# A weight set-up moved into the recurrence's first chunk, a router moved between expert products, and a reciprocal written to PSUM, in an eight-stage hybrid model on one core

## The chip, the cores and the metric

The program runs on one core of a Trainium2 chip, as one launch. The metric is the device time of one execution in microseconds (us), lower is better. Names used below: PE is TensorE, DVE is VectorE, ACT is ScalarE, POOL is GpSimd, SP is SyncE, which issues most DMAs.

## The reference

One sequence of 2048 tokens with 128 features, float32, goes through eight residual stages, each of the form `x = x + f(layernorm(x))`:

```
x = x + rwkv6(ln(x))              # 16 heads of 8: gated linear recurrence over 2048 steps
x = x + moe_top2(ln(x))           # 8 experts, hidden 256, exact gelu, b2 per expert
x = x + rope_attention(ln(x))     # causal, 16 heads of 8
x = x + moe_top2(ln(x))           # the same weights again
x = x + full_attention(ln(x))     # 1 head of 128, not causal
x = x + perturbed_ffn(ln(x))      # 8 experts, 7 of them alike, softmax router
x = x + latent_attention(ln(x))   # causal, 8 heads of 128 over 2 latents of 32
x = x + perturbed_ffn(ln(x))
```

The top-2 router is `softmax((h @ Wg + bg) / 5)`, the two largest kept and divided by their sum. The perturbed weights need the k-th smallest and largest absolute value of four tensors.

## The kernel before, in words

Tokens lie in 16 tiles of 128 (`NT`), or 4 chunks of 512 (`NC`, `CH`). X stays in SBUF for the whole program. Each stage is a class with one method for each engine; `build` makes a list of stages, and each engine runs its method of stage after stage in that list. So an engine's instructions stand in the order of the list, and engines meet only at semaphores. PSUM has eight banks, which the stages share by number (`k.bank(7)`).

**The recurrence** (`Rwkv`) goes over the 4 chunks and in each over 8 columns j. DVE makes a product with the replicated values (`kvj`), a scan (`state`) and a product with r (`rsj`); PE replicates the values for column j + 2 and sums `rsj` into bank 6. At j = 5 PE also projects the next chunk. Bank 7 serves the group norm of the chunk before (centre, variance, spread, output), and is not used in chunk 0. ACT copies the projections out (`take`), with a change of table between sigmoid and exp.

**Later weights** (`LaterWeights`) prepare what later stages read: 15 transposes of 128 x 128 on PE (the qkv weights, the padded output weights, `wq`), two small ones, and the products `wc` and `wy`; ACT copies each group from PSUM. DVE splits the rows of b2 into three bfloat16 parts on three partitions (`split_rows`) and makes four strided copies for the rotated qkv weights. In the list this stage stands behind the recurrence, so every engine comes to it when the recurrence is done. DVE's layer norm of the first expert stage stands behind it. GpSimd's part of it runs early, at 32 us, and GpSimd then waits for the recurrence to end, and starts a bisection of 31 rounds (`Perturb`) that runs beside the next stages.

**Experts** (`Experts`, `Router`). In each chunk PE does, for e = 0 to 7, the hidden products of expert e (2 products, banks 0 to 3) and the output of expert e - 1 (a seed from the b2 rows, then 8 products, banks 4 and 5). ACT applies gelu. DVE adds the gated output to X. The router stands ahead of that as its own stage: 16 narrow products into bank 7, then some two dozen small DVE instructions and one exp on ACT, to the gates. PE waits until DVE has read the logits before it goes on.

**Latent attention** (`CausalHeads` with `summed`). A plan made at build time interleaves on PE the scores of key tile after key tile with "ring" items, which pass through banks 5 to 7: maxima ahead of time, turns, sums, outputs. DVE works the ring items in the same order. The softmax denominators are sums over keys of exp(scores): for each unit GpSimd adds the weights of heads 0 to 2 to an accumulator in SBUF, DVE those of head 3 (line 1533). At the end of each of the 8 (quad, chunk) pairs PE sums the accumulator over partitions into a ring bank, DVE takes the reciprocal (line 1641) into SBUF, and multiplies it with the output `O` (line 1643).

The profile counts lines of this kernel: 202, 221, 227 layer norm; 468 to 485 later weights on PE; 495 to 505 their copies on ACT; 516, 524 to 530 the DVE part; 737, 792, 809 the recurrence on DVE; 989, 994, 1001 hidden, seed and output products; 1053 the gated addition; 1085 the router's products; 1375, 1611 maxima.

Of the kernel before, what the change touches and what calls it, by code (L numbers as in the profile page):

```python
# [22 lines left out]
P = 128  # L23
# [232 lines left out]
class Setup(Stage):  # L256
# [43 lines left out]
    def alloc(self, ctx):  # L300
# [14 lines left out]
        self.row0 = sb("row0", [3, 8, P])  # L315
        self.rowr = sb("rowr", [3, 8, P])
        self.rowb = sb("rowb", [3, 8, P], BF16)
        self.n_loaded, self.n_rest = (16 * len(x) for x in self.loads())

    def loads(self):  # L320
# [29 lines left out]
        load(self.row0[:, :, :], d["L0_ffn_b2"].rearrange("(a e) d -> a e d", a=1).broadcast_to([3, 8, P]))  # L350
# [79 lines left out]
class LaterWeights(Stage):  # L430


    def __init__(self, k):
        self.k, self.setup = k, k.setup
        self.turned = self.setup.turned
        self.copied = [k.sem(f"later_copied{i}") for i in range(2)]
        self.ready = k.sem("later_ready")


    def groups(self):  # L440
        k, s = self.k, self.setup
        pads = [s.wpad[:, g, :, :].rearrange("p j c -> p (j c)") for g in range(4)]
        return [([s.wraw[:, i, :] for i in range(5, 8)], k.wqkvT[:, 0:3, :]),
                (pads, k.woutT[:, :, :]), ([s.wq[:, i, :] for i in range(4)], s.wqT[:, 0:4, :]),
                ([s.wq[:, i, :] for i in range(4, 8)], s.wqT[:, 4:8, :])]

    def gpsimd(self, g):
        k, s = self.k, self.setup
        g.wait_ge(s.loaded_rest, s.n_rest)
        g.wait_ge(s.loaded, s.n_loaded)  # L450
        g.wait_ge(s.zeroed, s.n_zeroed)
        g.tensor_copy(s.wpad[:, :, :, 0:8], s.wraw[:, 8, :].rearrange("p (g j d) -> p g j d", g=4, j=4)) \
            .then_inc(self.ready, 1)
        g.tensor_copy(k.identb[:, :], k.ident).then_inc(self.ready, 1)
        g.tensor_copy(k.mask_qk[:, :], k.cst[:, (5 + 8) * P:(6 + 8) * P]).then_inc(self.ready, 1)
        g.tensor_copy(k.mask_kq[:, :], k.cst[:, (6 + 8) * P:(7 + 8) * P]).then_inc(self.ready, 1)

    def tensor(self, pe):
        k, s = self.k, self.setup
        pe.wait_ge(s.loaded_rest, s.n_rest)  # L460
        pe.wait_ge(s.ready, 1)
        pe.wait_ge(self.ready, 4)
        n = 0
        for ins_, _ in self.groups():
            if n >= 2:
                pe.wait_ge(self.copied[n % 2], n // 2)
            for i, a in enumerate(ins_):
                ins = pe.transpose(k.PS[:, 4 + n % 2, i * P:(i + 1) * P], a, k.ident)
            ins.then_inc(self.turned[n % 2], 1)
# [12 lines left out]

        for h in range(8):
            g, j = h // 4, h % 4
            ins = pe.matmul(k.PS[32 * j:32 * j + 32, 4, g * P:(g + 1) * P], s.wvupT[:, :], s.wo[:, h, :],
                            start=True, stop=True)
        ins.then_inc(self.turned[0], 1)

    def scalar(self, act):
        k, s = self.k, self.setup  # L490
        n = 0
        for _, out in self.groups():
            act.wait_ge(self.turned[n % 2], n // 2 + 2)
            w = out.shape[1]
# [1725 lines left out]
```

## Time and profile before

| | us |
|---|---|
| median of 3 runs | 1803.63 |
| the runs | 1799.49, 1803.63, 1818.74 |
| the profiled execution | 1799.15 |
| its span, first to last instruction | 1797.3 |

The stages in the trace: set-up and recurrence to 161.5 us, first experts 161.5 to 326, rope attention to 880, second experts to 1030, full attention to 1230, first perturbed experts to 1340, latent attention to 1711, second perturbed experts to the end. Over the span PE is busy 1578.2 us, DVE 1127.0, ACT 772.4, POOL 753.4. A share of the whole span says little here, since each stage has its own limit; a change is read in its own stage. A granted clock of 1.00 is 2.4 GHz on TensorE, 0.50 is 1.2 GHz.

### The profile page before, as it was taken

The numbers are of one execution on the slowest core, as the hardware profiler recorded it, in microseconds if no ns is written. First come the engines' busy times: TensorE is split into PE (matmuls) and PEld (weight loads), VectorE is DVE, ScalarE is ACT, GpSimd is POOL, SyncE is SP. The second block draws the span as 40 slices with busy tenths as digits, with TensorE's granted clock in tenths as the row PEclk, the third lists the DMA queues.
The fourth block names the chain that finished last, engine by engine and source line by source line (L and its number), as shares of the span: only waits on it lengthen the run. The fifth ranks groups of instructions, "written<-read, shape, count | busy, mean of one in ns | idle before, by whom it ended". The sixth has DMA issues, their size and how long they took to land.

```text
span 1797.3 us, 25837 instructions
## 1 busy us (share of the span) xinstructions
PE 1578.2 (88%) x8927; PEld 810.0 (45%) x8927; DVE 1127.0 (63%) x2330; ACT 772.4 (43%) x1007; POOL 753.4 (42%) x955
## 2 busy tenths in 40 slices
PE   5885999689999899999799879989879889898689
PEld 2333666333333344343366547776634333333256
DVE  6778333798788787884233333334378978787941
ACT  2321333615565555656433334444344334344443
POOL 0003636454554536363645454600004546667800
PEclk9997899859999999999799989997979889899879
DMA  5000000323001010000000000000062000000000
GB/s 149 0 1 1 1 1 0 116 55 54 2 16 41 2 45 12 2 2 2 1 1 1 0 0 1 0 0 1 0 183 56 23 23 2 1 0 2 0 7 18
DMA packets 39124, 36.90 MB, mean 21 GB/s; under 512 B 10190, under 2 KB 36271, under 8 KB 38898
## 3 DMA queue, kind: packets, MB, share of 16 engines
q1 hardware_dynamic: 36826, 28.48, 5.6%
q10 hardware_dynamic: 2136, 7.10, 2.0%
q8 instruction: 62, 1.02, 0.2%
q14 instruction: 36, 0.29, 0.1%
q0 software_dynamic: 64, 0.00, 0.0%
HBM read 26.10 MB, written 8.91 MB: 19 GB/s over the span
## 4 chain that ended last, share of the span: by engine, by line
PE 70%; DVE 14%; issue 3%; ACT 3%; POOL 2%; DMA 1%; SPq 0%; DVEq 0%; POOLq 0%; ACTq 0%
PE PS L1427 11%; PE PS L1001 10%; PE PS L1375 10%; PE PS L1446 10%; PE PS L989 10%; PE PS L1875 3%; PE PS L1893 3%; DVE sb_rope_mp L1611 3%; POOL sb_H L1533 2%; DVE sb_latent_mp L1611 2%; DVE sb_latent_rec L1641 1%; PE PS L1887 1%; PE PS L994 1%; PE PS L1085 1%; PE PS L1404 1%
## 5 line engine op out<-in xcount | busy, mean ns | idle before, releaser
L1611 DVE TENSOR_REDUCE sb_rope_mp<-PS 128x1 f32<-128x512 f32 (+3 forms) x560 | 344.5, 668 | 67.7 <-PE PS L1379 33.3
L1488 ACT ACTIVATE sb_rope_PT<-PS 128x1024 f32<-128x1024 f32 (+3 forms) x320 | 273.3, 895 | 212.3 <-PE PS L1431 114.2
L1053 DVE SCALAR_TENSOR_TENSOR sb_X<-PS,sb_gates,sb_X 128x128 f32 (+1 forms) x320 | 90.2, 344 | 238.4 <-PE PS L1001 238.2
L1375 PE MATMUL PS<-sb_rope_K,sb_rope_Q 96*128 96x512 bf16 (+3 forms) x640 | 212.8, 372 | 7.6 <-ACT sb_rope_V L1473 6.5
L1611 DVE TENSOR_REDUCE sb_latent_mp<-PS 128x1 f32<-128x512 f32 (+2 forms) x280 | 175.6, 668 | 36.7 <-PE PS L1375 26.9
L593 POOL TENSOR_SCALAR sb_pbelow<-sb_pa,sb_ptrial 128x512 f32<-128x512 f32 x124 | 194.0, 1575 | 6.4
L600 POOL TENSOR_TENSOR sb_pbelow<-sb_pbelow 128x1024 f32<-128x1024 f32 (+1 forms) x248 | 182.4, 735 | 19.6
L989 PE MATMUL PS<-sb_HT,sb_w 128*128 (+1 forms) x384 | 181.9, 611 | 3.6 <-DVE sb_seed L528 1.9
L1427 PE MATMUL PS<-sb_rope_Q,sb_rope_K 99*128 99x512 bf16 (+3 forms) x640 | 181.1, 354 | 1.4 <-ACT sb_rope_PT L1488 0.9
L1427 PE MATMUL PS<-sb_latent_Q,sb_latent_K 96*128 96x512 bf16 (+7 forms) x640 | 158.8, 369 | 5.3 <-ACT sb_w0b L1488 2.4
L1030 ACT ACTIVATE sb_moe_hidden<-PS,sb_vec 128x512 f32<-128x512 f32 x128 | 87.5, 687 | 158.7 <-PE PS L989 154.6
L1446 PE MATMUL PS<-sb_rope_PT,sb_rope_V 128*9 128x512 f32 (+3 forms) x1280 | 150.0, 541 | 0.1
L1375 PE MATMUL PS<-sb_latent_K,sb_latent_Q 96*128 96x512 bf16 (+3 forms) x320 | 106.8, 382 | 30.7 <-DVE sb_latent_mp L1611 22.6
L1375 PEld LDWEIGHTS PS<-sb_rope_K,sb_rope_Q 96*128 96x128 bf16 x640 | 59.9, 100 | 161.8 <-issue 83.2
L1001 PE MATMUL PS<-sb_w0b,sb_moe_hidden 128*128 128x128 f32 x1024 | 131.3, 281 | 0.0
L1001 PEld LDWEIGHTS PS<-sb_w0b,sb_moe_hidden 128*128 128x128 f32 x1024 | 119.1, 191 | 14.5 <-issue 14.5
L989 PEld LDWEIGHTS PS<-sb_HT,sb_w 128*128 128x128 f32 x384 | 70.2, 197 | 69.5 <-issue 65.5
L606 POOL TENSOR_TENSOR sb_ptot<-sb_ptot,sb_prank 128x8 f32<-128x8 f32 x31 | 6.1, 197 | 223.0 <-issue 223.0
L1427 PEld LDWEIGHTS PS<-sb_latent_Q,sb_latent_K 99*128 99x128 bf16 (+1 forms) x640 | 58.2, 102 | 82.3 <-issue 20.7
L605 POOL PARTITION_ALL_REDUCE sb_ptot<-sb_pcnt x31 | 13.2, 426 | 187.2 <-issue 187.2
L1427 PEld LDWEIGHTS PS<-sb_rope_Q,sb_rope_K 99*128 99x128 bf16 x640 | 59.3, 100 | 69.7 <-issue 18.3
L1531 POOL COPY sb_pbelow<-sb_w 128x1536 f32<-128x1536 f32 x3 | 4.4, 1462 | 189.6 <-ACT sb_w L1488 181.9
(322 smaller groups left out, 2622.3 us busy)
## 6 DMA issues: line engine op xcount, KB each, us to landing
sb_latent_Q<-latent_parts SPq DMA_DIRECT2D x48, 128.0 KB, 2.8
sb_rope_Q<-rope_parts ACTq DMA_DIRECT2D x9, 384.0 KB
rope_parts<-sb_rope_parts SPq DMA_DIRECT2D x24, 128.0 KB, 2.4
latent_parts<-sb_latent_parts SPq DMA_DIRECT2D x12, 256.0 KB, 2.7
sb_rope_tab<-in_rotation SPq DMA_DIRECT2D x1, 2048.0 KB, 8.2
sb_rope_K<-rope_parts ACTq DMA_DIRECT2D x6, 256.0 KB
latent_parts<-sb_latent_parts SPq DMA_DIRECT2D x12, 128.0 KB, 2.4
sb_latent_K<-latent_parts SPq DMA_DIRECT2D x48, 32.0 KB, 2.2
```

What stands on the lines that cost most here:

```text
L593: ch.mark(g.tensor_scalar(self.below[:, w, s, :], self.a[:, w, :], tr[:, 2 * w + s:2 * w + s + 1], None, ALU.is_lt))
L600: ch(g.tensor_tensor(bl[:, :, 0:n], bl[:, :, 0:n], bl[:, :, n:2 * n], ALU.add))
L989: pe.matmul(k.bank(b), self.w1(e, m), x, start=True, stop=True).then_inc(self.hid[b], 1)
L1001: ins = pe.matmul(k.PS[:, 4 + b, i * P:(i + 1) * P], self.g[:, b, m, i * P:(i + 1) * P], self.w2(e, m), start=False, stop=(m == M - 1), sk ...
L1030: s.activation(self.g[:, e % 2, m, :], k.bank(b), self.func, bias=self.b1(e, m)) \
L1053: ins = v.scalar_tensor_tensor(xi, k.PS[:, 4 + b:5 + b, i * P:(i + 1) * P], gate, xi, ALU.mult, ALU.add)
L1375: ins = pe.matmul(k.PS[:, bank, at:at + w], self.Q[0:self.rows, g % 2, j, 0, q0:q0 + P], self.K[0:self.rows, g % 2, j % self.kheads, 0, kc ...
L1427: ins = pe.matmul(k.PS[:, j, q0:CH], self.K[0:r, g % 2, j % self.kheads, m, kj * P:(kj + 1) * P], self.Q[0:r, g % 2, j, m, c * CH + q0:(c ...
L1446: ins = pe.matmul(k.PS[32 * j:32 * j + self.vcols, 4, q0:CH], v, self.PT[u % self.B][:, j, q0:CH], start=(kj == 0), stop=(kj == last))
L1488: s.activation(self.PT[u % self.B][:, 2 * p:2 * p + 2, q0:CH], k.PS[:, 2 * p:2 * p + 2, q0:CH], ACT.Exp, scale=self.scale).then_inc(self.e ...
L1611: v.tensor_reduce(self.mp[:, n % 2, kc, heads[0]:heads[-1] + 1, i], k.PS[:, bank, 0:len(heads) * w].rearrange("p (h k) -> p h k", h=len(he ...
L1875: ins = pe.matmul(k.bank(c), self.qi[:, b, :], self.kT[:, c * CH:(c + 1) * CH], start=True, stop=True)
```

## The change

It has three parts.

1. **Later weights.** The stage is now ahead of the recurrence in the list, but has no PE, ACT or DVE method of its own. The recurrence calls `turn(pe, n)` and `copy(act, n)` in chunk 0: groups 0 to 3 on PE behind the columns 2 to 5, group 4 (`wc` and `wy`) behind column 7; ACT copies groups 0 to 3 ahead of `take(1)` and group 4 behind it. All go through bank 7, so each group waits for the copies of the one before, and the centring of chunk 1 waits for the last copy. The rotated qkv weights come from two more ACT copies. The b2 rows are split on GpSimd (5 instructions on 8 partitions) and brought to their three partitions by three DMAs from GpSimd's queue; the experts wait for these.
2. **Router.** In the two top-2 stages the router's products stand inside the experts' first turn on PE, behind the hidden products of expert 1, and its exp on ACT behind the gelus of expert 1. The wait for the logits to be read is gone.
3. **Latent reciprocal.** It is written over its own input in PSUM, and the multiplication reads it there. The bank is given back behind the multiplication, not behind the reciprocal.

```diff
 class LaterWeights(Stage):
+    FIRST = 5
+    LAST = 2
...
+    def before_group(self, n):
+
+        return 0 if n == 0 else self.FIRST + n - 1
+
+    @property
+    def all_copied(self):
+        return self.before_group(4) + self.LAST
 
     def gpsimd(self, g):
...
+        ch(g.tensor_copy(s.rowb[:, 0, :], s.row0[:, :]))
+        ch(g.tensor_tensor(s.row0[:, :], s.row0[:, :], s.rowb[:, 0, :], ALU.subtract))
+        ch(g.tensor_copy(s.rowb[:, 1, :], s.row0[:, :]))
+        ch(g.tensor_tensor(s.row0[:, :], s.row0[:, :], s.rowb[:, 1, :], ALU.subtract))
+        ch(g.tensor_copy(s.rowb[:, 2, :], s.row0[:, :]))
+        for r in range(3):
+            g.dma_start(k.seed0[r:r + 1, :, :], s.rowb[:, r, :]).then_inc(self.seeded, 16)
...
+    def turn(self, pe, n):
+        k, s = self.k, self.setup
+        if n == 0:
+            pe.wait_ge(s.loaded_rest, s.n_rest)
+        else:
+            pe.wait_ge(self.copied, self.before_group(n))
+        if n == 1:
+            pe.wait_ge(self.padded, 1)
+        if n == 4:
+            pe.wait_ge(self.padded, 4)
+        if n < 4:
...
+            for i, a in enumerate(blocks):
+                ins = pe.transpose(k.PS[:, 7, i * P:(i + 1) * P], a, k.ident)
...
+        ins.then_inc(self.turned, 1)
...
-    def vector(self, v):
-        k, s, ch = self.k, self.setup, Chain(v, self.setup.steps, self.setup.STEPS)
-        v.wait_ge(s.loaded_rest, s.n_rest)
-        split_rows(ch, v, s.row0[:, :, :], s.rowr[:, :, :], s.rowb[:, :, :], k.seed0[:, :, :], k)
-        v.wait_ge(self.copied[0], 1)
-
-        for i in range(2):
             for a in range(2):
-                ch(v.tensor_copy(k.wqkvT[:, 3 + i, :].rearrange("p (m a) -> p m a", a=2)[:, :, a:a + 1],
-                                 k.wqkvT[:, i, :].rearrange("p (m a) -> p m a", a=2)[:, :, 1 - a:2 - a]))
+                act.activation(k.wqkvT[:, 3:5, :].rearrange("p i (m a) -> p i m a", a=2)[:, :, :, a:a + 1],
+                               full[:, 0:2, :].rearrange("p i (m a) -> p i m a", a=2)[:, :, :, 1 - a:2 - a],
+                               ACT.Copy).then_inc(self.copied, 1)
...
@@ Rwkv.scalar, the end
             if c:
                 centre(c)
                 deviation(c)
+            else:
+                for n in range(4):
+                    k.later.copy(s, n)
             if c + 1 < NC:
                 take(c + 1)
+            if c == 0:
+                k.later.copy(s, 4)
@@ Rwkv.tensor
             pe.wait_ge(self.o_sb, m)
             if m > 1:
                 pe.wait_ge(self.ready, m - 1)
+            else:
+                pe.wait_ge(k.later.copied, k.later.all_copied)
...
+                if c == 0 and 2 <= j <= 5:
+                    k.later.turn(pe, j - 2)
+                if c == 0 and j == 7:
+                    k.later.turn(pe, 4)
@@ Experts
-        if not self.between:
-            for sem, val in self.router.banks_free():
-                pe.wait_ge(sem, val)
...
+                if first and e == 1 and not self.between:
+                    self.router.project(pe)
...
+                if first and e == 1 and not self.between:
+                    self.router.exponents(s)
@@ CausalHeads.dve_item, "sum", summed
-                v.reciprocal(self.rec[:, :], k.bank(bank)).then_inc(free, 1)
-                v.wait_ge(free, uses + 1)
-                v.tensor_tensor(self.On[:, n % 2, :], self.O[:, n % 2, :], self.rec[:, :], ALU.mult) \
-                    .then_inc(self.normed, 1)
+                ch(v.reciprocal(k.bank(bank), k.bank(bank)))
+                ch(v.tensor_tensor(self.On[:, n % 2, :], self.O[:, n % 2, :], k.bank(bank), ALU.mult))
+                v.sem_inc(self.normed, 1)
+                v.sem_inc(free, 1)
```

TensorE at the end of chunk 0 and the start of chunk 1 of the recurrence, before (`wvrep` are the value products, `rsj` the sums, `centring` and `sq` the group norm, `rk` the bonus):

```order
L890 MATMUL PS<-sb_rw_mixv,sb_wvrep 128x512
L938 MATMUL PS<-sb_rw_rsj,sb_cst 128x512
L890 MATMUL PS<-sb_rw_mixv,sb_wvrep 128x512
L938 MATMUL PS<-sb_rw_rsj,sb_cst 128x512
L896 MATMUL PS<-sb_rw_o,sb_centring 128x512
L901 MATMUL PS<-sb_cst,sb_rw_sq 128x16 x4
L928 MATMUL PS<-sb_rw_rk,sb_cst 128x512
```

The same place now:

```order
L896 MATMUL PS<-sb_rw_mixv,sb_wvrep 128x512
L946 MATMUL PS<-sb_rw_rsj,sb_cst 128x512
L896 MATMUL PS<-sb_rw_mixv,sb_wvrep 128x512
L946 MATMUL PS<-sb_rw_rsj,sb_cst 128x512
L492 MATMUL PS<-sb_wkupT,sb_wqT 128x32 x8
L495 MATMUL PS<-sb_wo,sb_wvupT 32x128 x8
L904 MATMUL PS<-sb_rw_o,sb_centring 128x512
L909 MATMUL PS<-sb_cst,sb_rw_sq 128x16 x4
L936 MATMUL PS<-sb_rw_rk,sb_cst 128x512
```

Sixteen products have come ahead of the centring; they stood behind the whole recurrence before.

TensorE from the end of the recurrence to the second expert, before (`rw_z` is the recurrence's last output, `wraw` to `wo` the later weights, `H` the layer norm's transposes, `wg` the router):

```order
L914 MATMUL PS<-sb_wT,sb_rw_z 128x128 x4
L468 MATMUL PS<-sb_cst,sb_wraw 128x128 x3
L468 MATMUL PS<-sb_cst,sb_wpad 128x128 x4
L468 MATMUL PS<-sb_cst,sb_wq 128x128 x8
L474 MATMUL PS<-sb_cst,sb_wup 128x32 x2
L480 MATMUL PS<-sb_wkupT,sb_wqT 128x32 x8
L485 MATMUL PS<-sb_wo,sb_wvupT 32x128 x8
L238 MATMUL PS<-sb_cst,sb_H 128x128 x16
L1085 MATMUL PS<-sb_wg,sb_HT 128x8 x16
L989 MATMUL PS<-sb_HT,sb_w 128x512 x4
L994 MATMUL PS<-sb_seed,sb_onesb 128x512
L1001 MATMUL PS<-sb_w0b,sb_moe_hidden 128x128 x8
```

And now:

```order
L922 MATMUL PS<-sb_wT,sb_rw_z 128x128 x4
L238 MATMUL PS<-sb_cst,sb_H 128x128 x16
L998 MATMUL PS<-sb_HT,sb_w 128x512 x4
L1108 MATMUL PS<-sb_wg,sb_HT 128x8 x16
L1003 MATMUL PS<-sb_seed,sb_onesb 128x512
L1010 MATMUL PS<-sb_w0b,sb_moe_hidden 128x128 x8
```

The later weights are gone from here, and the router and the first four hidden products have changed places.

VectorE around the second denominator of latent attention, now (`mp` are maxima, `pbelow` the accumulator of head 3):

```order
L1631 TENSOR_REDUCE sb_latent_mp<-PS 128x1 x2
L1661 RECIPROCAL PS<-PS 128x512
L1662 TENSOR_TENSOR sb_latent_On<-sb_latent_O,PS 128x512
L1631 TENSOR_REDUCE sb_latent_mp<-PS 128x1 x2
L1553 TENSOR_TENSOR sb_pbelow<-sb_pbelow,sb_w 128x512
L1631 TENSOR_REDUCE sb_latent_mp<-PS 128x1 x4
```

The order is that of before; the reciprocal's output and the multiplication's second input are in PSUM.

## Rows read from the trace of the kernel before

**Rows 1.** The page: its span, and the chain's shares by engine.

```profile
span 1797.3 us, 25837 instructions
...
PE 70%; DVE 14%; issue 3%; ACT 3%; POOL 2%; DMA 1%; SPq 0%; DVEq 0%; POOLq 0%; ACTq 0%
```

**Rows 2.** Timeline, VectorE, layer norms and recurrence's tail: start, duration, engine, line, operation.

```profile
13.98 4.19 DVE L227 TENSOR_SCALAR sb_H<-sb_X,sb_mv,sb_rstd 128x128 f32<-128x128 f32 x16
...
160.82 0.69 DVE L769 TENSOR_TENSOR sb_X<-sb_X,PS 128x512 f32<-128x512 f32 x1 [2.16 <-PE PS L914]
161.42 0.67 DVE L524 CAST sb_rowb<-sb_row 3x1024 bf16<-3x1024 f32 x1
...
171.88 0.87 DVE L202 BATCH_NORM_STATS2 sb_stats<-sb_X 128x6 f32<-128x128 f32 x4
...
174.48 6.06 DVE L227 TENSOR_SCALAR sb_H<-sb_X,sb_mv,sb_rstd 128x128 f32<-128x128 f32 x16
```

**Rows 3.** Timeline, the recurrence's chunks 0 and 1, then the later weights.

```profile
31.95 1.22 POOL L454 CAST sb_identb<-sb_cst 128x128 bf16<-128x128 f32 x1
...
58.74 1.12 PE L896 MATMUL PS<-sb_rw_o,sb_centring 128*128 128x512 f32 x2 [0.78 <-DVE sb_rw_o L742]
...
64.56 0.69 DVE L737 TENSOR_TENSOR sb_rw_kvj<-sb_rw_k,PS 128x512 f32<-128x512 f32 x1 [0.83 <-PE PS L890]
...
162.96 0.66 PE L468 MATMUL PS<-sb_cst,sb_wq 128*128 128x128 f32 x4 [0.24 <-ACT sb_woutT L495]
...
164.48 2.65 PE L480 MATMUL PS<-sb_wkupT,sb_wqT 128*128 128x32 f32 x16 [0.63 <-ACT sb_wvupT L500]
...
167.06 1.08 PE L485 MATMUL PS<-sb_wo,sb_wvupT 128*32 128x128 f32 x16
167.16 0.38 ACT L502 ACTIVATE sb_wc<-PS 128x256 f32<-128x256 f32 x1 [2.74 <-PE PS L480]
```

**Rows 4.** Timeline, the first expert stage's start.

```profile
182.40 6.99 PE L1085 MATMUL PS<-sb_wg,sb_HT 128*128 128x8 f32 x32 [0.69 <-ACT sb_HT L250]
...
189.78 5.23 PE L989 MATMUL PS<-sb_HT,sb_w 128*128 128x512 f32 x8 [0.38 <-DVE sb_rt_p L1102]
...
197.42 1.13 DVE L1053 SCALAR_TENSOR_TENSOR sb_X<-PS,sb_gates,sb_X 128x128 f32<-128x128 f32 x4
...
202.97 0.38 PE L994 MATMUL PS<-sb_seed,sb_onesb 3*128 3x512 bf16 x1
```

**Rows 5.** By line: count, duration ns min/median/max, first and last start, shape.

```profile
L1641 DVE RECIPROCAL sb_latent_rec<-PS x8: 3357/3357/3358, 1370.4 to 1704.0; 128x512 f32<-128x512 f32 x8
...
L1643 DVE TENSOR_TENSOR sb_latent_On<-sb_latent_O,sb_latent_rec x8: 691/3289/3800, 1373.8 to 1707.4; 128x512 f32<-128x512 f32 x8
...
L1652 DVE TENSOR_TENSOR sb_X<-sb_X,PS x24: 676/687/689, 436.8 to 1710.3; 128x512 f32<-128x512 f32 x24
```

**Rows 6.** Windows, latent attention: length, busy us of PE, PEld, DVE, ACT, POOL, granted clock.

```profile
1340.00:1711.00 371.00, 317.00 (x1937) 125.01 (x1935) 311.45 (x423) 147.53 (x170) 222.52 (x80) 0.90 0.06 18
```

**Rows 7.** Timeline, GpSimd and VectorE at the second and seventh denominators.

```profile
1393.30 3.42 POOL L1533 TENSOR_TENSOR sb_pbelow<-sb_pbelow,sb_w0b 128x1536 f32<-128x1536 f32 x1 [1.37 <-ACT sb_w0b L1488]
1393.47 3.80 DVE L1643 TENSOR_TENSOR sb_latent_On<-sb_latent_O,sb_latent_rec 128x512 f32<-128x512 f32 x1
...
1398.39 0.68 DVE L1533 TENSOR_TENSOR sb_pbelow<-sb_pbelow,sb_w 128x512 f32<-128x512 f32 x1
...
1659.36 3.95 POOL L1533 TENSOR_TENSOR sb_H<-sb_H,sb_w0b 128x1536 f32<-128x1536 f32 x1 [2.56 <-ACT sb_w0b L1488]
```

**Rows 8.** Windows (columns as in the group of latent attention); the sum is of five low stretches.

```profile
1393.90:1397.90 4.00, 0.04 (x1) 0.00 (x0) 4.00 (x3) 0.00 (x0) 2.82 (x1) 0.99 0.00 0
...
1656.60:1658.30 1.70, 0.04 (x4) 0.00 (x0) 1.67 (x3) 1.05 (x2) 0.19 (x1) 1.00 0.00 0
...
1397.90:1404.60 6.70, 6.67 (x23) 2.18 (x23) 5.55 (x13) 2.05 (x2) 0.24 (x1) 0.50 0.00 0
...
sum 30.90, PE 30.68 PEld 10.16 DVE 22.42 ACT 9.10 POOL 5.61; mean PE 6.14 PEld 2.03 DVE 4.48 ACT 1.82 POOL 1.12
```

More of the change, by code:

```diff
@@ L430 @@
 class LaterWeights(Stage):
+    FIRST = 5
+    LAST = 2
     def __init__(self, k):
         self.k, self.setup = k, k.setup
[L435 to L445, printed above, removed]
+        k.later = self
+        self.turned = k.sem("later_turned")
+        self.copied = k.sem("later_copied")
+        self.padded = k.sem("later_padded")
+        self.pool_steps = k.sem("later_steps")
+        self.seeded = k.sem("later_seeded")
+    def before_group(self, n):
[3 more added lines that the diff above has]
+        return self.before_group(4) + self.LAST
     def gpsimd(self, g):
-        k, s = self.k, self.setup
+        k, s, ch = self.k, self.setup, Chain(g, self.pool_steps)
         g.wait_ge(s.loaded_rest, s.n_rest)
@@ new lines, in copy @@
+    def copy(self, act, n):
+        k, s = self.k, self.setup
+        act.wait_ge(self.turned, n + 1)
+        full = k.bank(7).rearrange("p (n d) -> p n d", d=P)
+        if n == 0:
+            act.activation(k.wqkvT[:, 0:3, :], full[:, 0:3, :], ACT.Copy).then_inc(self.copied, 1)
+            for a in range(2):
+                act.activation(k.wqkvT[:, 3:5, :].rearrange("p i (m a) -> p i m a", a=2)[:, :, :, a:a + 1],
+                               full[:, 0:2, :].rearrange("p i (m a) -> p i m a", a=2)[:, :, :, 1 - a:2 - a],
+                               ACT.Copy).then_inc(self.copied, 1)
+            act.activation(s.wkupT[:, :], k.PS[:, 7, 384:416], ACT.Copy).then_inc(self.copied, 1)
+            act.activation(s.wvupT[:, :], k.PS[:, 7, 416:448], ACT.Copy).then_inc(self.copied, 1)
+        elif n < 4:
+            out = (k.woutT[:, :, :], s.wqT[:, 0:4, :], s.wqT[:, 4:8, :])[n - 1]
+            act.activation(out, full, ACT.Copy).then_inc(self.copied, 1)
+        else:
+            act.activation(k.wc[:, :, :], k.PS[:, 7, 0:256].rearrange("p (h l) -> p h l", h=8), ACT.Copy) \
+                .then_inc(self.copied, 1)
+            act.activation(k.wy[:, :, :], k.PS[:, 7, 256:512].rearrange("p (h l) -> p h l", h=2), ACT.Copy) \
+                .then_inc(self.copied, 1)
@@ L1021, in scalar, with turn @@
         uses = E * M // 4
-        for sem, val in self.needs:
-            s.wait_ge(sem, val)
-        def turn(c):
+        if self.between:
+            for sem, val in self.needs:
+                s.wait_ge(sem, val)
+        def turn(c, first):
             for e in range(E):
@@ L1036, in scalar @@
         with s.Fori(1, NC) as c:
-            turn(c)
+            turn(c, False)
     def vector(self, v):
@@ L1081, in tensor, with scalar, project @@
     def tensor(self, pe):
+        if not self.inside:
+            self.project(pe)
+    def scalar(self, s):
+        if not self.inside:
+            self.exponents(s)
+    def project(self, pe):
         k = self.k
@@ L2106, in rwkv @@
             perturb.after = [(rw.ready, NC)]
[L2107 removed]
+            stages.extend([SetupCopies(k), LaterWeights(k), rw])
             return lambda c: [(rw.ready, c + 1)]
[L2110 to L2113 removed]
         def full_attention():
```

93 lines of the change are left out of this document (29 added, 64 removed).

## The prediction

> **What bounds the kernel.** I read the first lines of the page, then the chain of waits, then the stretches that the change touches as timelines, and the granted clock of a few short windows. The profiled execution took 1799.15 us for a span of 1797.3; the median of the three runs is 1803.63, so the sum below stands 4.5 under it. The chain that ended last is TensorE for 70% of the span and VectorE for 14% [rows 1]. Three stretches matter. At the end of the recurrence VectorE alone holds up the next stage: from the last addition to X to the next statistics it does twelve instructions that the next stage doesn't need [rows 2]. In the first expert stage TensorE does the router, then the hidden products. In latent attention both TensorE (317 of 371 us) and VectorE (311 of 371) are nearly full [rows 6], so there a shorter VectorE instruction can count.
>
> **1. The tail of the recurrence.** The last addition ends at 160.82 + 0.69 = 161.5, the statistics start at 171.88 [rows 2]. Between them stand the split of b2 and four copies. The change takes both from VectorE, and the statistics wait for nothing else: 10.4 us gone. TensorE's turns and ScalarE's copies lay beside them and go too. What is late next is the normalization itself.
> Given back, a: chunk 0. Four groups of about four transposes go in after j = 2 to 5, each about 0.66 us [rows 3]. VectorE sets the pace in chunk 0, and TensorE waits for it ahead of its products, so two or three groups are covered; the last stands right ahead of chunk 1's projections, behind which VectorE is the one that waits. I take one group uncovered, +0.7 (bounds 0 and 4 x 0.66 = 2.6).
> Given back, b: the last group, after j = 7: 2.65 + 1.08 us of products, then two ScalarE copies of 0.38, and the centring of chunk 1 now waits for these [rows 3]. TensorE was idle 0.78 there. 3.73 + 0.7 - 0.8 = +3.6. Behind the waiting centring stand the variance, the bonus and the value products, and VectorE already waits 0.83 us for those, so it passes through in full. Bounds: 2.0 (products at the full clock) and 5.
> Given back, c: the normalization now meets GpSimd's opening instructions. Its sixteen instructions took 4.19 us with GpSimd idle and 6.06 beside it [rows 2]; I take +1.5 on top (bounds 0 and 4).
> The b2 rows: five GpSimd instructions on 8 partitions and three DMAs on GpSimd's queue. No row shows them. The nearest is the cast of the identity, 1.22 us beside VectorE [rows 3]; eight of these, 10 us, from 31.7 on are over long before the last group at 58, and the experts need the result after 160. Nothing for it; at 3 us each they would start to hold the group. They may delay VectorE in chunk 0 by up to 0.5 us, within bound a.
> Part 1: -10.4 + 0.7 + 3.6 + 1.5 = **-4.6** (-8.4 to +1.7).
>
> **2. The router inside turn 0**, twice. Before: router 6.99 us, a wait of 0.38, hidden products 5.23, first gated addition 197.42 - 182.40 = 15.0 us after the start [rows 4]. Now the hidden products come first, and the logits come that much later: with 6.0 for the products (the clock is still low) and 4.5 for the router (between half of 6.99 and all of it), at 10.5 instead of 7.0. VectorE's chain from logits to the first addition stays 197.42 - 182.40 - 6.99 = 8.0, so the addition ends at 10.5 + 8.0 + 1.1 = 19.6. The first TensorE instruction that needs it, the seed of expert 2, began 20.6 us after the start (202.97) [rows 4]. So there is 1 us of slack and 0.38 saved. Against it stands the clock: the router's narrow products come just ahead of expert 0's, and where the clock falls behind them each stretch of 4 us costs 2. ScalarE has one more table load, beside the router. I take **+1.5** for both (-3 to +6), nearer the zero that the slack gives.
>
> **3. The latent reciprocal in PSUM.** The reciprocal takes 3.357 us in all eight cases. The multiplication behind it, both inputs in SBUF, has a median of 3.289 and a least value of 0.691; the addition of an SBUF tile and a PSUM bank of the same size takes 0.676 to 0.689 in all 24 cases [rows 5]. The timeline shows why: GpSimd starts an addition at 1393.30, and VectorE's multiplication of 0.69 runs from 1393.47 until that has ended [rows 7]. Once one input is in PSUM I expect 0.69 each time: 3.289 - 0.687 = 2.6 us of VectorE at each of five chunks, some 0.5 at the first, where GpSimd's instruction is short, nothing at the last, where GpSimd is done. No row shows a reciprocal that writes PSUM; its 3.357 for 512 columns, five times a plain instruction, says the arithmetic sets it. Bounds: 3.36 and twice that.
> How much of the 2.6 arrives? The next but two VectorE instruction is its own head's addition, again with two SBUF inputs (1398.39) [rows 7]. With the multiplication short, two maxima (1.27) run inside GpSimd's 3.42 us, and that addition then waits in its place: 1393.30 + 3.42 + 0.7 = 1397.4, against an end at 1399.07 before. Arrives: 1.7. Five chunks: -8.5 (up to -13).
> The Trainium skill, page SBUF — State Buffer, section Who interferes with whom, has this as a lock: a VectorE instruction with two SBUF inputs and a GpSimd instruction that reads SBUF exclude each other, and one with at most one SBUF input does not contend. The 24 even additions agree; the same rule moves the wait to the next such instruction, so it speaks for 1.7, not 2.6.
> At the seventh chunk VectorE's late copy left GpSimd idle for 2.56 us, and from there to the end GpSimd sets the pace [rows 7]: -2.6 (1.5 at least).
> The clock: at such a chunk TensorE was idle for 4.0 us, and then ran 6.7 us at 1.2 GHz [rows 8]. Five such stretches sum to 30.9 us; at 2.4 GHz their TensorE work would save 15.5, but VectorE was busy 22.4 of them, which leaves 8.5. With maxima freed early the idle time should shrink to 1 to 2 us, and a gap of 1.7 us left the clock at 1.00 [rows 8]. I take -7 (0 to -15.5).
> The bank is free 0.75 us later than before; two others are full then, so nothing.
> Part 3: -0.5 - 8.5 - 2.6 - 7 = **-18.6** (-10.5 to -31).
> The Trainium skill, TensorE: Matmul & The Clock Gate, Part 1, says that activity releases a throttle and idleness brings it back; that the clock would then stay up is its reading too, and it would give the whole 8.5.
>
> **Sum:** 1799.15 - 4.6 + 1.5 - 18.6 = 1777.5. The profiled execution lies at the low end of its runs, so I say 1779.
>
> **Rivals.**
> A, the forecast, 1779 (own range 1771 to 1786): 0.44.
> B, all arrives: the next addition doesn't meet GpSimd, the clock stays up: latent -27, so 1799.15 - 4.6 + 1.5 - 27 = 1769. For it: VectorE is nearly full there. Against: the addition two maxima later. 0.20.
> C, the wait only moves: 1.7 per chunk, and TensorE, stopped by the moved wait, still falls to 1.2 GHz: latent -10.5, 1785.5, with the usual offset 1787. This is the lock of the skill's SBUF page taken to its end. 0.27.
> D, the change doesn't do what it says: the multiplication waits for GpSimd even with an input in PSUM: 1796. The 24 additions speak against it: they reach from 436.8 to 1710.3 us, and GpSimd is busy 222.5 of the 371 us of latent attention. 0.03.
> E, slower: the reciprocal reading and writing one bank takes twice its 3.36 us. It lies on the chain at each chunk: 8 x 3.36 = 27, so 1777.5 + 27 = 1804.5. It decides from about 2.7 us more per reciprocal on; no row of before writes PSUM from an arithmetic VectorE instruction. 0.06.
>
> **Numbers.** Range 1762 to 1794: it holds A and C, and most of B. 1% of 1803.63 is 18 us, about what a measurement of this kernel can tell from no change. Below 1785.6: nearly all of B, 0.33 of A's 0.44, 0.08 of C: 0.61. Slower by over 1% (above 1821.7) needs E with the upper bounds of parts 1 and 2: 0.03. The rest, 0.36, is within 1%.
>
> **What would show it.** The multiplication in latent attention at 0.69 us eight times, the reciprocal at 3.36; a two-SBUF addition of about 2 us some 2 us behind it; fewer windows at clock 0.50 between 1390 and 1600; statistics right behind the last addition of the recurrence; VectorE's wait at chunk 1 of the recurrence (0.83) grown to about 5 us; the first gated addition some 18.5 us after the normalization. Wrong would be a TensorE that waits as long at each latent chunk as before, a normalization of 8 us beside GpSimd, or a reciprocal of another length.

## The result, and the profile after

The change is a little faster: the median of 19 runs is 1787.31 us (1778.68 to 1797.82) against 1799.49 us (1793.79 to 1818.74) of 19 runs of the kernel before, 12.2 us between the medians, and a ratio of 0.9929 (95% interval 0.991 to 0.9948). The interval doesn't reach 1, so the gain is real, but it is under 1%. The forecast was 1779, against a profiled execution of 1799.15, from a sum of -21.6 us.

The profiled execution of the change took 1797.82 us, the slowest of the 19. Its total says little; its stages do. The page, where [rows 1] was:

```profile
span 1796.0 us, 25854 instructions
...
PE 69%; DVE 17%; issue 2%; ACT 2%; DMA 1%; SPq 1%; DVEq 0%; ACTq 0%
```

The timeline of the change around the end of the recurrence and the first expert stage (columns as in [rows 2]):

```profile
163.98 0.69 DVE L770 TENSOR_TENSOR sb_X<-sb_X,PS 128x512 f32<-128x512 f32 x1 [2.17 <-PE PS L922]
164.80 0.87 DVE L202 BATCH_NORM_STATS2 sb_stats<-sb_X 128x6 f32<-128x128 f32 x4
...
167.41 6.78 DVE L227 TENSOR_SCALAR sb_H<-sb_X,sb_mv,sb_rstd 128x128 f32<-128x128 f32 x16
...
176.09 5.35 PE L998 MATMUL PS<-sb_HT,sb_w 128*128 128x512 f32 x8 [0.73 <-issue]
181.28 3.63 PE L1108 MATMUL PS<-sb_wg,sb_HT 128*128 128x8 f32 x32
...
186.62 6.33 POOL L601 TENSOR_TENSOR sb_pbelow<-sb_pbelow 128x1024 f32<-128x1024 f32 x8
186.88 2.23 DVE L1131 TENSOR_TENSOR sb_rt_p<-sb_rt_p,sb_rt_a 128x128 f32<-128x128 f32 x1
189.15 1.25 DVE L1138 COPY sb_rt_left<-sb_rt_p 128x128 f32<-128x128 f32 x1
...
197.50 0.39 PE L1003 MATMUL PS<-sb_seed,sb_onesb 3*128 3x512 bf16 x1 [2.88 <-DVE sb_X L1067]
```

The statistics stand right behind the last addition: 164.80 instead of 171.88. The normalization is stretched a little more than in [rows 2]. The seed of expert 2 comes 21.4 us behind the stage's first product (20.6 in [rows 4], where that is the router's) and waits 2.88 us for the gated addition, because two instructions of VectorE's gate chain, 0.29 and 0.23 us when alone, took 2.23 and 1.25 beside GpSimd's additions.

At the boundary of chunks 0 and 1 (as [rows 3]), on TensorE and then VectorE:

```profile
58.31 1.87 PE L492 MATMUL PS<-sb_wkupT,sb_wqT 128*128 128x32 f32 x16
60.11 0.64 PE L495 MATMUL PS<-sb_wo,sb_wvupT 128*32 128x128 f32 x16
...
66.81 0.69 DVE L738 TENSOR_TENSOR sb_rw_kvj<-sb_rw_k,PS 128x512 f32<-128x512 f32 x1 [2.57 <-PE PS L896]
```

VectorE's wait is 2.57 us instead of 0.83. In latent attention, by line and at the second denominator (as [rows 5] and [rows 7]):

```profile
L1661 DVE RECIPROCAL PS<-PS x8: 3366/3366/3367, 1384.2 to 1701.1; 128x512 f32<-128x512 f32 x8
...
L1662 DVE TENSOR_TENSOR sb_latent_On<-sb_latent_O,PS x8: 686/686/687, 1387.6 to 1704.5; 128x512 f32<-128x512 f32 x8
```

```profile
1407.17 0.69 DVE L1662 TENSOR_TENSOR sb_latent_On<-sb_latent_O,PS 128x512 f32<-128x512 f32 x1
1408.11 1.29 DVE L1631 TENSOR_REDUCE sb_latent_mp<-PS 128x1 f32<-128x512 f32 x2 [0.25 <-DVE sb_latent_On L1662]
1409.31 1.67 DVE L1553 TENSOR_TENSOR sb_pbelow<-sb_pbelow,sb_w 128x512 f32<-128x512 f32 x1
...
1408.08 0.39 PE L1395 MATMUL PS<-sb_latent_K,sb_latent_Q 96*128 96x512 bf16 x1 [1.10 <-DVEq L1664]
```

A reciprocal that writes PSUM costs 0.01 us more, the multiplication 0.69 all eight times, and VectorE's own addition behind two maxima takes part of the wait over: 1.67 instead of 0.68. TensorE stood still for 1.10 us here, where it had stood for 4.0 [rows 8].

Now the stages, from the start of one stage's first new statistics to the next's (for latent attention from 0.7 us ahead of them, in all three). Windows of before, of the change, and of the change in a second profiled execution (columns as in [rows 6]): rope attention, the second experts, latent attention.

```profile
321.90:880.70 558.80, 509.33 (x3328) 199.78 (x3328) 426.19 (x795) 312.23 (x371) 283.22 (x469) 0.93 0.12 28
880.70:1027.70 147.00, 140.04 (x720) 90.60 (x720) 55.14 (x201) 50.61 (x73) 77.72 (x129) 0.95 0.00 0
1295.70:1711.30 415.60, 346.47 (x2064) 141.06 (x2064) 343.51 (x508) 166.33 (x207) 222.52 (x80) 0.89 0.11 31
```

```profile
316.40:888.80 572.40, 517.59 (x3328) 201.84 (x3328) 434.11 (x795) 312.41 (x371) 286.39 (x476) 0.92 0.12 27
888.80:1040.50 151.70, 138.78 (x720) 89.77 (x720) 58.00 (x201) 51.89 (x74) 76.41 (x130) 0.94 0.00 0
1311.70:1708.50 396.80, 338.17 (x2064) 138.41 (x2064) 332.57 (x507) 166.64 (x207) 223.29 (x80) 0.91 0.11 33
```

```profile
323.90:886.70 562.80, 512.43 (x3328) 199.52 (x3328) 432.36 (x795) 312.58 (x371) 284.38 (x469) 0.93 0.12 28
886.70:1031.40 144.70, 137.75 (x720) 90.02 (x720) 53.27 (x201) 51.72 (x74) 78.07 (x129) 0.96 0.00 0
1300.20:1702.40 402.20, 340.52 (x2064) 139.50 (x2064) 335.10 (x508) 166.81 (x207) 222.88 (x80) 0.91 0.11 32
```

Latent attention gave 13 to 19 us. Rope attention, which the change doesn't touch, took 4 to 14 us more, and the second experts differ by 7 us between two executions of one kernel; 4.2 of the 7 is their normalization, 9.15 us in one and 4.97 in the other. These are what the experiments had to explain.

### The profile page after: what moved, and what is told of

Its sections match the earlier page's. It is cut to its first block, busy times and chain, and to the rows that moved or that the text cites. A ratio compares the mean times of both kernels' runs of the same rounds, so it can differ in the third digit from the quotient of the medians.

```text
span 1796.0 us, 25854 instructions
## 1 busy us (share of the span) xinstructions
PE 1575.2 (88%) x8927; PEld 808.4 (45%) x8927; DVE 1122.6 (63%) x2318; ACT 775.8 (43%) x1011; POOL 756.6 (42%) x963
## 4 chain that ended last, share of the span: by engine, by line
PE 69%; DVE 17%; issue 2%; ACT 2%; DMA 1%; SPq 1%; DVEq 0%; ACTq 0%
PE PS L1447 11%; PE PS L1466 10%; PE PS L1395 10%; PE PS L1010 10%; PE PS L998 9%; PE PS L1895 3%; PE PS L1913 3%; DVE sb_H L1553 3%; DVE sb_rope_mp L1631 2%; DVE sb_latent_mp L1631 2%; DVE sb_H L227 2%; DVE PS L1661 1%; PE PS L1907 1%; PE PS L1003 1%; PE PS L1424 1%
```

## The experiments

Ratios are to runs of the kernel before on the same chip. That kernel's median moved between these batches and chips, from 1799.49 ahead to 1806.87, 1802.02, 1801.13 and 1805.68 us, while the change itself took 1787.31 and 1786.22; so a ratio carries up to 0.4% that its interval doesn't show, and totals of different batches are compared with care. Stage times are read from one profiled execution each.

**Each part alone, and the whole again.** `weights_alone` is part 1, `router_alone` part 2, `latent_alone` part 3 of the diff ahead; `changed_again` is unedited.

> Only the first part (later weights in chunk 0), router and latent reciprocal as before. Theory S (the parts add up, and the 17.9 us more at 1.2 GHz in rope attention are the luck of one execution): the next statistics begin at 164 to 166 us instead of 171.9, the first expert stage gains 3 to 6 us, rope attention takes 559 us within 8, total 3 to 6 us below before. Theory W (part 1 itself slows rope attention, because work reaches it at another point): rope attention near 572 us here too, total above before by 5 us or more.

> Only the second part (router behind the hidden products of expert 1). Theory S: the seed of expert 2 waits for the first gated addition, 21 us after the normalization instead of 20.6 in the first expert stage and 19 in the second: total 0 to 2 us above before. Theory R (the router inside the turn is worth its 7 us of TensorE): total 5 us or more below before. Theory W2 (the second table load and the late gates cost both stages): 5 us or more above.

> Only the third part (reciprocal written to PSUM). Theory S: latent attention 12 to 18 us shorter than the 371.3 of before (355.5 in the whole change), total 10 to 17 us below before, that is nearly the whole of what the change gave. Theory C (the wait only moves and the clock falls as before): latent attention 361 us, total 8 us below. In both, eight reciprocals of 3.36 us and eight multiplications of 0.69.

> The whole change again, unedited, for another execution's profile. Theory S (luck of one execution): median 10 to 16 us below before, and in this profile rope attention takes less than the 572.5 us of the first, by 5 us or more, with fewer us at 1.2 GHz than 96. Theory W: rope attention 570 to 575 us again.

| kernel | median us | ratio | 95% interval |
|---|---|---|---|
| weights_alone | 1805.57 | 0.9973 | 0.9937 to 1.0008 |
| router_alone | 1801.97 | 0.9976 | 0.9937 to 1.0014 |
| latent_alone | 1787.34 | 0.9883 | 0.983 to 0.9937 |
| changed_again | 1786.22 | 0.9864 | 0.9826 to 0.9902 |

Part 3 gives nearly all of it; parts 1 and 2 can't be told from nothing by the time. Latent attention took 402.1 us in `latent_alone` and 402.2 in `changed_again` (expected by S: 12 to 18 less than before, read: 13.5 less). The medians of these two lie 20 us below that batch's kernel before, more than S said (10 to 17 and 10 to 16); most of the excess is that kernel's slower batch.

For `router_alone` the interval of the total reaches down to 11 us below before, so the time alone leaves theory R open. The profile speaks against it: the first expert stage took 147.7 us (150.0 before), the second 148.9 (147.0), and 7 us were gained in neither. Nor was there the wait that theory S expected: the seed of expert 2 waited for nothing, and the gate chain took its old 7.9 us.

For `weights_alone` the total speaks against theory W (the interval ends 1.4 us above before). Its profiled execution took 1821.08 us, the second slowest of twelve, so its 571.0 us for rope attention decide nothing. W's doubt about that stage stays: rope attention took 562.8 us in `changed_again`, less than 572.4, but more than the 558.4 and 560.5 of the two kernels without part 1.

The two levels of latent attention, 396.8 and 402.2, have one visible origin. `changed_again`, GpSimd and VectorE behind the second denominator, then TensorE:

```profile
1404.87 2.90 POOL L1553 TENSOR_TENSOR sb_pbelow<-sb_pbelow,sb_HT 128x1536 f32<-128x1536 f32 x1 [3.76 <-ACT sb_HT L1508]
1404.94 2.87 DVE L1647 TENSOR_TENSOR sb_latent_negp<-sb_latent_neg,sb_latent_negp 128x16 bf16<-128x16 f32 x1
...
1408.46 1.56 PE L1424 MATMUL PS<-sb_wy,sb_latent_On 128*128 128x128 f32 x8 [3.07 <-DVE sb_latent_mp L1631]
```

An instruction on 16 columns, 0.17 us when alone, began 0.07 us behind a GpSimd addition and waited for all of it; TensorE stood still for 3.07 us and then ran at 1.2 GHz for some us. In the change's first profile it was through in 0.17, and the interval between the second and third reciprocal was 35.5 us instead of 38.8. That is 3.3 of the 5.4 us; the other 2.2 lie ahead of the first reciprocal (72.5 against 74.7 us), where part 3 has not yet acted. The wait is no rarity: `latent_alone` and `gpsimd_held` have the same 2.87 us and 38.8, while `changed_g4`, `combined` and `held_three_router_ahead` have 35.5.

**The last group elsewhere.** `changed_g4`:

```diff
-                if c == 0 and j == 7:
+                if c == 1 and j == 2:
                     k.later.turn(pe, 4)
...
-                pe.matmul(k.PS[:, 7, h * 32:(h + 1) * 32], s.wqT[:, h, :], s.wkupT[:, :], start=True, stop=True)
+                pe.matmul(k.PS[:, 3, h * 32:(h + 1) * 32], s.wqT[:, h, :], s.wkupT[:, :], start=True, stop=True)
```

The group's two copies on ScalarE move with it, and the projection of chunk 2 waits for them.

> The whole change, but the last group of later weights (wc and wy) goes behind column 2 of chunk 1, through bank 3, which lies idle there; the centring of chunk 1 no longer waits for its copies. Theory G (the group sits on the path at the chunk boundary for 2.3 us and is covered at column 2): VectorE's wait for the values of chunk 1 falls from 2.57 us to 0.2 to 0.9, and the total is 2 to 3 us below the change's. Theory G0 (what is saved there is waited for at the next boundary, where VectorE or ScalarE sets the pace): the same total as the change within 1 us.

1784.93 us, ratio 0.99 (0.9843 to 0.9956). Locally, on VectorE and TensorE:

```profile
67.40 0.69 DVE L739 TENSOR_TENSOR sb_rw_kvj<-sb_rw_k,PS 128x512 f32<-128x512 f32 x1 [0.79 <-PE PS L899]
...
73.41 1.87 PE L493 MATMUL PS<-sb_wkupT,sb_wqT 128*128 128x32 f32 x16
75.21 0.65 PE L496 MATMUL PS<-sb_wo,sb_wvupT 128*32 128x128 f32 x16
...
76.94 0.69 DVE L739 TENSOR_TENSOR sb_rw_kvj<-sb_rw_k,PS 128x512 f32<-128x512 f32 x1 [0.99 <-PE PS L899]
```

The wait at the boundary falls by 1.78 us, and 0.99 of it comes back where the 2.5 us of products now stand: column 2 covers 1.5 of 2.5. So 0.8 us, which the total can't show. Theory G was right in the place and some three times too large in the sum.

**GpSimd held.** `gpsimd_held` puts GpSimd's 31 rounds behind the normalizations:

```diff
+            if len(perturb.after) == 2:
+                perturb.held.append((ln.mem.normed, ln.chunk_ready(NC - 1)))
+            else:
+                perturb.after.append((ln.mem.normed, ln.chunk_ready(NC - 1)))
...
+        rounds(22)
+        for sem, val in self.held:
+            g.wait_ge(sem, val)
+        rounds(9)
```

> The whole change, but GpSimd's bisection starts only when the first expert stage's normalization is done, and after 22 of 31 rounds it waits for the second expert stage's normalization. Theory P (a normalization beside GpSimd's instructions is stretched, and by how much hangs on where in its round of 30.5 us GpSimd is; 4.2 us without it, up to 9.2 beside its additions): the first two expert normalizations take 4.19 us each (6.8 and 5.0 to 9.2 in the change), the total is 3 to 7 us below the change's. Theory Q (the normalization is hidden by something else, or GpSimd then ends too late): no gain, or a wait before the first perturbed experts.

`combined` has this edit and the one before.

> The whole change with both edits: the last group at column 2 of chunk 1, and GpSimd held at the two normalizations. If both theories G and P hold: 5 to 9 us below the change, 0.5% at the most; if one of them fails, that much less.

1791.71 us, 0.9917 (0.9878 to 0.9956), and 1785.49 us, 0.9882 (0.9817 to 0.9947): no gain that can be told. The normalizations say why. Of the change (second experts, with GpSimd's additions beside it), then of `gpsimd_held` (first experts, start of rope's, second experts):

```profile
891.45 9.15 DVE L227 TENSOR_SCALAR sb_H<-sb_X,sb_mv,sb_rstd 128x128 f32<-128x128 f32 x16
895.10 6.34 POOL L601 TENSOR_TENSOR sb_pbelow<-sb_pbelow 128x1024 f32<-128x1024 f32 x8
```

```profile
168.57 4.19 DVE L227 TENSOR_SCALAR sb_H<-sb_X,sb_mv,sb_rstd 128x128 f32<-128x128 f32 x16
...
315.56 5.15 DVE L227 TENSOR_SCALAR sb_H<-sb_X,sb_mv,sb_rstd 128x128 f32<-128x128 f32 x7
...
877.60 4.19 DVE L227 TENSOR_SCALAR sb_H<-sb_X,sb_mv,sb_rstd 128x128 f32<-128x128 f32 x16
```

Theory P holds for the two that were guarded; what they save does not show in the total. But GpSimd starts 8 us later now, and its additions fall on rope attention's normalization: all sixteen instructions took 8.6 us (4.2 in the change). Over the executions read, a normalization took 4.2 us when it began 17.6 to 24 us into GpSimd's round of some 30.5 (counted from the round's second instruction), 4.2 to 5.0 at 26.5 to 27.6, 5.4 at 2.7, and 8.4 to 9.2 at 4.4 to 7.1. The long ones are not part 1's doing alone: `latent_alone`, without it, had 8.95 us in the second experts.

**Both inputs in SBUF, GpSimd nearly idle.** `gpsimd_no_sums` leaves out nearly all of GpSimd's sums:

```diff
+            if who == 0:
+                new, acc = (a[:, heads, CH - 4:CH] for a in (self.PT[u % self.B], self.acc[n % 2]))
             eng.tensor_tensor(acc, acc, new, ALU.add).then_inc(self.added[who], 1)
```

> The kernel before, its latent reciprocal in SBUF; of the sums of heads 0 to 2 in latent attention GpSimd adds only the last 4 columns of each head (the rest is left out). Theory L (VectorE's multiplication waits for GpSimd's running instruction): the multiplication takes 0.7 us all eight times although both its inputs are in SBUF, the head-3 additions 0.68, and latent attention, from the norm to the last addition to X, is shorter than the 399.6 us of the change by 5 us or more, since no such wait is left. Theory M (SBUF inputs themselves make it 3.3 us): still 3.3 us.

```profile
L1645 DVE TENSOR_TENSOR sb_latent_On<-sb_latent_O,sb_latent_rec x8: 691/692/711, 1372.9 to 1653.9; 128x512 f32<-128x512 f32 x8
```

1748.16 us, 0.9709 (0.9649 to 0.9769). Theory L: the multiplication takes 0.69 us out of SBUF too, so it was GpSimd that it waited for. From the norm to the last addition, latent attention took 360.8 us, against 413.1 before and 399.7 in `changed_again`. GpSimd's sums, by VectorE's waits and at the end by GpSimd's own pace, cost up to 52 us, and the change took away 13.

**Who adds.** `one_adder`:

```diff
-            self.add_weights(g, u, 0, slice(0, 3))
+            self.add_weights(g, u, 0, slice(0, 4))
...
-                if item == "weighted" and self.summed:
-                    self.add_weights(v, u, 1, slice(3, 4))
-                elif item[0] == "reciprocals":
+                if item[0] == "reciprocals":
```

> The whole change, but in latent attention GpSimd adds the weights of all four heads to the accumulator and VectorE none. Theory L (VectorE's two-SBUF additions of head 3 take over the wait that the multiplication lost, and hold up its maxima): without them VectorE has no instruction left there that waits for GpSimd, latent attention falls below the 399.6 us of the change by 5 to 20 us. Theory A (GpSimd becomes the bound: its instructions get 4/3 as long, 223 us become some 300 of 371, and the denominators wait for it at each chunk's end): latent attention 5 to 20 us longer than the change's.

1796.48 us, 0.9952 (0.9919 to 0.9984); from the norm to the last addition 406.6 us. In the sum theory A, in the parts both. Theory L's premise, that VectorE would have nothing left that waits, did not hold: an instruction on 16 columns took 4.36 us beside a GpSimd addition, and a cast later 4.35.

```profile
1487.71 4.53 POOL L1551 TENSOR_TENSOR sb_pbelow<-sb_pbelow,sb_w0b 128x2048 f32<-128x2048 f32 x1
1487.91 4.36 DVE L1641 TENSOR_TENSOR sb_latent_neg<-sb_latent_neg,sb_latent_negp 128x16 f32<-128x16 f32 x1
```

Intervals between the eight reciprocals, before, in the two profiles of the change, here, and in the last experiment:

| | 1-2 | 2-3 | 3-4 | 4-5 | 5-6 | 6-7 | 7-8 |
|---|---|---|---|---|---|---|---|
| before | 19.67 | 38.48 | 41.85 | 58.77 | 55.03 | 63.69 | 56.10 |
| the change | 19.56 | 35.49 | 37.51 | 54.77 | 53.09 | 61.99 | 54.52 |
| changed_again | 19.56 | 38.81 | 37.47 | 54.77 | 53.07 | 62.00 | 54.48 |
| one_adder | 18.67 | 32.94 | 35.43 | 55.34 | 55.08 | 64.52 | 63.38 |
| heads_split | 18.70 | 32.94 | 35.45 | 56.20 | 48.73 | 61.82 | 48.61 |

**Rope's normalization guarded too, and the router back.** `held_three` is `combined` with a third wait; `held_three_router_ahead` has the router as before.

```diff
-        rounds(22)
+        rounds(4)
+        for sem, val in self.held0:
+            g.wait_ge(sem, val)
+        rounds(18)
         for sem, val in self.held:
...
+            perturb.held0 = [(ln.mem.normed, ln.chunk_ready(NC - 1))]
```

> The combined kernel, in which GpSimd also waits for rope attention's normalization after 4 rounds (4, 18, 9 instead of 22, 9). Theory P: the normalizations of both expert stages and of rope attention take 4.2 to 5 us each (4.2, 8.5, 4.2 in the combined kernel), and the total is 2 to 6 us below the combined kernel's, 22 to 28 below before. Theory Q: what the rope stage saves at its start it waits for later: no difference to the combined kernel.

> The kernel held_three with the router ahead of the experts as before. Theory S (the router inside the turn is worth nothing within 2 us, for the seed of expert 2 waits for the gates): the same total within 3 us. Theory R (with GpSimd out of the way VectorE's gate chain is short enough and the router inside pays): 3 to 8 us above held_three.

1775.72 us, 0.9818 (0.9771 to 0.9864), and 1771.69 us, 0.9783 (0.973 to 0.9836). All three normalizations took 4.19 us in both. Rope attention took 560.5 and 560.8 us, though part 1 is in. That GpSimd's three waits made the whole faster than the change is likely, not shown: the interval of `held_three` (up to 0.9864) overlaps those of `combined` and `changed_again`. The router inside is worth nothing: the seed of expert 7 began 39.5 us behind the end of the normalization in both stages of `held_three`, and 38.9 and 38.6 with the router ahead. Theory S; the totals, 4 us apart with overlapping intervals, add nothing.

**The best version.** `heads_split` is the last one with

```diff
+    def pool_heads(self, u):
+        n = self.chunk(*self.unit(u)[:2])
+        return 4 if n < 4 else 2 if n == 7 else 3
...
+                    if self.pool_heads(u) < 4:
+                        self.add_weights(v, u, 1, slice(self.pool_heads(u), 4))
+                    else:
+                        v.sem_inc(self.added[1], 1)
```

> The kernel held_three_router_ahead, in which the heads whose weights GpSimd adds in latent attention hang on the chunk: all four in the first four (quad, chunk) pairs, three in the next three, two in the last; VectorE adds the rest. Theory L + A (in the early pairs VectorE's wait for GpSimd is the cost, in the last pair GpSimd's own pace; all heads on GpSimd changed the intervals of the first pairs by -0.9, -3 to -6 and -2.0 us, and those of the late ones by +2.0, +2.5 and +8.9): intervals of the second to fourth pair as in one_adder (18.7, 33, 35.4 us), the last below 54.5 by 4 to 8 us; latent attention 6 to 14 us shorter than 398, the total 6 to 14 us below held_three_router_ahead, about 1762. If the whole gain of the early pairs in one_adder was the clock's luck: only the last pair gains, 4 to 8 us.

1762.07 us (1753.2 to 1765.57), ratio 0.9742 (0.9688 to 0.9796): faster than the kernel before and than the change, and not to be told by the total from the version that it edits (0.9783). The table has its intervals: the early ones as in `one_adder`, the last 5.9 us shorter than in `changed_again`. Interval 5-6 fell by 4.3 us too, which wasn't expected and isn't explained. From the norm to the last addition it took 384.1 us.

## Why the prediction came out as it did

**Direction and range were right, and so was the main mechanism; the sum was about twice too large, and the total landed where it did partly by luck.** 1787.3 lies in 1762 to 1794, but above A's own range (to 1786) and beside C's 1787. The medians are 12.2 us apart where 20 to 25 were forecast, so the gain is under 1%, for which the prediction gave 0.36, against 0.61 for more. The base was right: 19 runs of the kernel before have a median of 1799.49. By stage, us against the profile of before:

| term | forecast | first profile | `changed_again` |
|---|---|---|---|
| recurrence and its tail | -6.1 | -7.1 | +0.4 |
| normalization and router, first experts | +1.5 and +0.75 | +1.6 | +1.6 |
| rope attention | 0 | +13.6 | +4.0 |
| router, second experts | +0.75 | +4.7 | -2.3 |
| full attention, first perturbed experts | 0 | +3.2 | +0.8 |
| latent attention | -18.6 | -18.8 | -13.4 |
| last experts | 0 | +1.5 | +1.5 |
| sum | -21.6 | -1.3 | -7.4 |

Both executions are the slowest of their kernel's runs (1797.82 and 1791.77 us), so these sums fall short of the 12.2 us; what they show is where the time goes.

*The tail.* -10.4 as forecast. The uncovered group was 0.43 us for 0.7 (VectorE's wait ahead of the chunk's last sum 5.58 to 6.01). The group at the boundary, forecast at 3.6, was smaller: its products ran at 2.4 GHz and took 2.5 us, not 3.7, and VectorE's wait grew by 1.7, just under the lower bound of 2.0. These three make -8.2 where -7.1 was read; the rest isn't traced. In `changed_again` the products took 2.5 us too, but the clock had fallen behind them, and the same wait was 6.13 (in `gpsimd_held` 5.18); the recurrence ended at 171.5 then, 6.9 us later than in the first profile, 3.6 us of it by this wait and 2.8 by a set-up that had ended later. Over four executions with part 1 the recurrence stage took 164.8, 172.3, 166.0 and 166.1 us, over four without it 171.9, 170.6, 176.3 and 174.2: -6.0 between the means.

*The router.* Forecast +1.5 for two stages; with GpSimd held, 0.6 and 0.9. In the change itself the slack of 1 us was there on paper only. The step that missed: the gate chain was taken at its old 8.0 us, though it would run at another point of GpSimd's round; it took 11.3 us (184.95 to 196.28), the first gated addition began 22.1 us behind the normalization (forecast 18.5), and the slack became a wait of 2.88. It took 11.3 in `changed_again`, `changed_g4` and `one_adder` too, and 7.9 with no wait in `router_alone`. So it is not the router's new place that stretched it, but part 1, with which the stage meets GpSimd at another point.

*Latent attention.* The rule of the moved wait was right: the multiplications lost 16.1 us of duration over eight, and the head-3 additions gained 7.7 (77.1 to 84.8), most of it at the end, where GpSimd sets the pace. I had let it move to one place only. It also moves to instructions that nobody looks at: the tiny one of 2.87 us, which made of -3.0 us at the second denominator a +0.3. From the first to the eighth reciprocal the kernels with `rec` in SBUF took 333.6 us (`before`, `weights_alone` and `router_alone` within 0.1). Of the eight executions with it in PSUM and three heads on GpSimd, four took 316.9 (the first profile, `changed_g4`, `combined`, `held_three_router_ahead`, within 0.1) and four 320.2 (three with the tiny wait, and `held_three` without it). So part 3 is worth 13.4 or 16.7 us there, and the -18.8 that looks like the forecast holds 2.2 us of luck.

The sixteen-column casts that wait for GpSimd (1.09 to 2.27 us, four of eight) were there before and stayed. In the four intervals from the third denominator to the seventh the time shrank by 4.4, 4.0, 2.0 and 1.7 us. The first two got some clock back as well (granted 0.88 to 0.91 and 0.94), the other two only the moved wait, forecast at 1.7 (0.91 to 0.90 and 0.95 to 0.94). The fourth and fifth interval, before and in `changed_again` (columns as in [rows 6]):

```profile
1470.40:1529.20 58.80, 52.53 (x307) 20.76 (x306) 51.11 (x81) 22.37 (x25) 35.01 (x13) 0.88 0.01 1
1529.20:1584.20 55.00, 48.60 (x285) 18.55 (x284) 43.40 (x66) 22.34 (x25) 34.18 (x13) 0.91 0.00 1
```

```profile
1470.70:1525.50 54.80, 50.04 (x307) 19.99 (x307) 48.81 (x80) 22.49 (x25) 35.05 (x13) 0.94 0.01 2
1525.50:1578.60 53.10, 48.37 (x285) 18.34 (x284) 41.42 (x67) 22.36 (x25) 34.23 (x13) 0.90 0.00 1
```

Of the 5.2 us that are missing in `changed_again` 3.4 are the second interval (forecast 1.7 and a share of the clock, 3.1 in all), 1.0 the last (-1.6 for -2.6), and 0.4 the first (-0.1 for -0.5); the clock's term of -7, spread over five intervals, came in the others as far as that can be read.

The Trainium skill, page SBUF — State Buffer, section Who interferes with whom, says more than I took from it: casts, copies and tensor_scalar in a 2-port mode can contend as well, and whoever issues first has the ports for the whole instruction. The traces agree: the normalizations are tensor_scalar (4.19 us alone, 9.15 beside GpSimd), the casts have one input. In latent attention VectorE does two such casts and two small tensor_tensor instructions eight times over, besides the head-3 additions, so rival B needed the next of all these to miss GpSimd's addition.

*Rope attention.* Not in the forecast at all, and the largest miss. Read: with part 1 and GpSimd's rounds free it took 572.4, 562.8, 565.4 and 563.4 us in four executions of three kernels (the change twice, `changed_g4`, `one_adder`), without part 1 558.8, 558.4, 560.5 and 557.3, and with part 1 and three normalizations guarded 560.5, 560.8 and 557.4. VectorE was busy in it for 426.2 to 429.4 us without part 1, and 431.4 to 434.1 with it. In `gpsimd_held` and `combined` it took 562.1 and 566.8, of which 4.4 and 4.3 are the stretched normalization. This fits one cause, that part 1 brings the stage to another point of GpSimd's rounds, at some 7 us in the mean; no run varies that point alone, so it is argued, not shown. Not shown either: which instructions of the stage; and the 10 us between 562.8 and 572.4 in one and the same kernel go with time at 1.2 GHz (granted clock 0.93 and 0.92), whose place differs between executions with the same waits.

**Rivals.** B falls: its latent -27 was never seen, the best of all executions being some -19. C's total came, but not by C: latent attention gave 13.4 to 18.8 us, not 10.5, the clock fell less in some intervals and not in others, and the difference was lost in stages that C didn't name. D and E fall by the two rows of line 1661 and 1662.

## What to carry to other kernels

Where two engines lock each other out, price every instruction behind the one that is freed, down to the smallest, and every stage that the change moves in time against the other engine's loop. A loop with slack on the side engine can be made to wait at the few instructions that matter: here three waits brought three normalizations to 4.19 us. And read more than one profile before a stage's time is put down to a change: here -18.8 and -13.4 are the same kernel.

## What the runs showed of the hardware

- A reciprocal of 128 x 512 takes 3.357 us into SBUF and 3.366 into PSUM, over its own input.
- A VectorE instruction of 0.17 us waited 2.87 us for a GpSimd addition that had begun 0.07 us ahead of it.
- GpSimd on 8 partitions x 128 columns beside VectorE: casts 0.28 to 1.10 us, subtractions 0.82 and 1.26; all 5 done in 4.3 us, far below the forecast 10.
- One kernel in two executions took 164.8 and 172.3 us to the end of the recurrence and 151.7 and 144.7 for the second experts. In the first pair the clock had fallen at a chunk boundary (VectorE's wait 2.57 and 6.13 us), in the second the normalization met GpSimd's additions or missed them (9.15 and 4.97 us).
